# A local transformer's attention: squares of queries and keys in two operations, and the probabilities turned and emptied ahead of the values' projections

## The reference

```python
qkv = x @ Wqkv                              # shifted tokens
q = l2norm(q) * qs;  k = l2norm(k) * ksc    # t / max(norm(t), 1e-12), per head
q = q * cos * scale + rotate_half(q) * sin * scale
k = k * cos * inv   + rotate_half(k) * sin * inv
sim  = einsum('bhwie,bhwje->bhwij', q, look(k)) * 8.0   # this window and the one before
attn = softmax(where(mask, -max, sim), -1)
out  = einsum('bhwij,bhwje->bhwie', attn, look(v))
x = out @ Wo + x
# feed-forward, on shifted tokens again:
xn = (x - mu) / sqrt(var + 1e-05) * g + bln
a, gate = split(xn @ W1 + b1);  x = (a * gelu(gate)) @ W2 + b2 + x
```

## Time and profile before

| | |
|---|---|
| median of 3 runs | 2661.72 us (2658.05 to 2662.82) |
| the profiled execution | 2664.8 us |
| its span, first to last instruction | 2663.0 us |
| busy share of the span | PE 92%, PEld 73%, DVE 81%, ACT 74%, POOL 58% |
| mean granted clock of PE | 0.986 of full speed |

### The profile page before, as it was taken

How to read it: one execution, slowest core, us unless ns; L and a number is a source line. 1 busy time by engine, 2 the same in 40 slices (tenths; PEclk the granted TensorE clock), 3 DMA queues, 4 the chain that set the end, 5 groups by cost and what they waited for, 6 DMA issues and landing times. The chain is left out here.

```text
span 2663.0 us, 118331 instructions
## 1 busy us (share of the span) xinstructions
PE 2454.4 (92%) x52349; PEld 1956.3 (73%) x52349; DVE 2152.0 (81%) x2455; ACT 1983.5 (74%) x3935; POOL 1534.9 (58%) x1075
## 2 busy tenths in 40 slices
PE   6799999999999999999999999679999989997999
PEld 2478788888777788788887787557776767775787
DVE  5788888888788888888887787388888988885888
ACT  4678888888787888888887887566767666764776
POOL 3788887888778878887887777022223222322011
PEclk9899999999999999999999999899999999999999
DMA  3243433343334333434442333031322222221221
GB/s 95 55 93 90 104 76 91 90 105 79 88 89 104 76 91 92 106 78 95 93 107 62 83 83 80 25 72 36 74 52 66 46 64 53 62 49 37 81 71 42
DMA packets 275791, 201.99 MB, mean 76 GB/s; under 512 B 117568, under 2 KB 215880, under 8 KB 274248
## 3 DMA queue, kind: packets, MB, share of 16 engines
q1 hardware_dynamic: 275280, 194.42, 30.5%
HBM read 36.96 MB, written 1.11 MB: 14 GB/s over the span
## 5 line engine op out<-in xcount | busy, mean ns | idle before, releaser
L509 POOL TENSOR_TENSOR lt_t_sin<-lt_qk,lt_tab 128x512 f32<-128x512 f32 x384 | 685.0, 1804 | 261.2 <-DVE lt_qk L1274 258.7
L514 POOL TENSOR_TENSOR lt_qr<-lt_qr,lt_t_sin 128x1024 f32<-128x1024 f32 x192 | 455.7, 2373 | 28.7 <-PE bank L604 1.4
L2043 DVE TENSOR_REDUCE fa_neg_max<-bank 128x1 f32<-128x1024 f32 x256 | 301.5, 1219 | 94.1 <-PE bank L1851 93.4
L1267 DVE TENSOR_REDUCE lt_ssq<-lt_qr 128x32 f32<-128x2048 f32 x96 | 219.4, 2285 | 142.9 <-ACT lt_qr L976 142.9
L1875 PE MATMUL bank<-fa_prob_t,fa_v 32*64 32x128 f32 x16384 | 280.6, 275 | 31.0 <-issue 26.5
L2053 DVE STREAM_TRANSPOSE fa_prob_t<-fa_prob 128x1024 f32<-128x1024 f32 x256 | 302.0, 1218 | 0.0
L1875 PEld LDWEIGHTS bank<-fa_prob_t,fa_v 32*64 32x64 f32 x16384 | 242.5, 131 | 78.5 <-issue 57.2
L1965 ACT ACTIVATE fa_prob<-bank,fa_neg_max 128x1024 f32<-128x1024 f32 x128 | 142.5, 1114 | 207.8 <-DVE fa_neg_max L2043 161.6
L602 PE MATMUL bank<-lt_w_high,lt_x_high 128*128 128x512 f32 x576 | 280.4, 487 | 1.6 <-ACT lt_v_tok L995 1.3
L619 PE MATMUL bank<-ident,lt_qr 128*128 128x128 f32 x1536 | 234.6, 276 | 30.6 <-ACT lt_q_t L1010 18.9
L1274 DVE TENSOR_TENSOR lt_qk<-lt_qk,lt_rn 128x2048 f32<-128x2048 f32 x96 | 234.9, 2447 | 33.2 <-ACT lt_rn L989 32.3
(11 more groups left out here) (259 smaller groups left out, 5832.4 us busy)
## 6 DMA issues: line engine op xcount, KB each, us to landing
lt_v<-lt_v_tok SPq DMA_DIRECT2D x576, 128.0 KB, 2.4
fa_v<-fa_v_tok SPq DMA_DIRECT2D x256, 128.0 KB
lt_v<-lt_v_tok SPq DMA_DIRECT2D x192, 64.0 KB, 2.1
lt_k_t<-lt_k_t SPq DMA_DIRECT2D x84, 128.0 KB, 2.7
lt_v<-lt_v SPq DMA_DIRECT2D x168, 64.0 KB, 2.0
lt_w_raw<-in_lt_wqkv_dram SPq DMA_DIRECT2D x36, 256.0 KB, 3.6
ex_cw_all<-cw_kept SPq DMA_DIRECT2D x8, 1024.0 KB, 4.7
lt_x_s<-h_in SPq DMA_DIRECT2D x96, 64.0 KB, 2.8
```

Of the source, the lines that this page charges most:

```text
L509: pool.tensor_tensor(dst[:, :, i, :], src[:, :, 1 - i, :], tab[:, g // 2 % 2, 1, at:at + 32].unsqueeze(1).to_broadcast([P, HEADS, 32]), AL ...
L514: pool.tensor_tensor(qr[:, g % 2, half], qr[:, g % 2, half], t_sin[:, :], ALU.add).then_inc(S.rotated, 1)
L2043: dve.tensor_reduce(neg_max[:, u % 2, par:par + 1], bank[:, 2 * par:2 * par + 2, :].rearrange("p a n -> p (a n)"), AX.X, ALU.max, negate=T ...
```

## The change

On PE, both `turn_prob` of block i - 1 come right after `scores(i)`, ahead of both value projections, instead of between them. The table `uses` is reordered alike. On ACT, the square of the 2048 queries and keys of a block becomes two operations of 1024: the queries' half stands ahead of the emptying of the probabilities, the keys' half where the whole square was. The copy of the first values (`empty_v(i + 1, 0)`) moves behind the copies of the probabilities. The first half waits for the first two `qk` copies only and for the first two groups of turned `qr`; DVE's sum waits for both halves.

```diff
--- before.py
+++ after.py
@@ -275,13 +275,13 @@
                 uses["att", i - 2, 1] = len(uses)
             if i - 2 == ALL - 1:
                 uses["out", i - 2, 0] = len(uses)
+            if live(i - 1):
+                uses["prob", i - 1, 0] = len(uses)
+                uses["prob", i - 1, 1] = len(uses)
             if live(i + 1):
                 uses["v", i + 1, 0] = len(uses)
             if even(i, 6) is not None:
                 uses["down", even(i, 6), 0] = len(uses)
-            if live(i - 1):
-                uses["prob", i - 1, 0] = len(uses)
-                uses["prob", i - 1, 1] = len(uses)
             if live(i + 1):
                 uses["v", i + 1, 1] = len(uses)
             if even(i, 5) is not None:
@@ -919,6 +919,9 @@
                         last_mean(0)
                     if live(i):
                         scores(i)
+                    if live(i - 1):
+                        turn_prob(i - 1, 0)
+                        turn_prob(i - 1, 1)
                     if live(i + 1):
                         project_v(i + 1, 0)
                     if i == ALL + 2:
@@ -935,9 +938,6 @@
                     if i == ALL + 5:
                         last_mean(4)
                         last_var(4)
-                    if live(i - 1):
-                        turn_prob(i - 1, 0)
-                        turn_prob(i - 1, 1)
                     if live(i + 1):
                         project_v(i + 1, 1)
                     if live(i - 1):
@@ -969,11 +969,13 @@
                     act.wait_ge(S.proj, 4 * g + j + 1)
                     act.copy(qk[:, g % 2, j * CH:(j + 1) * CH], bank[:, turn_bank("qk", g, j), :]).then_inc(S.proj_out, 1)
 
-                def square_qk(g):
-                    act.wait_ge(S.proj_out, 4 * (g + 1))
+                def square_qk(g, a):
+
+                    half = slice(INNER * a, INNER * a + INNER)
+                    act.wait_ge(S.proj_out, 4 * g + 2 * a + 2)
                     if g >= 2:
-                        act.wait_ge(S.turned, 4 * (g - 1))
-                    act.activation(qr[:, g % 2, :], qk[:, g % 2, :], ACT.Square).then_inc(S.squared, 1)
+                        act.wait_ge(S.turned, 4 * (g - 2) + 2 * a + 2)
+                    act.activation(qr[:, g % 2, half], qk[:, g % 2, half], ACT.Square).then_inc(S.squared, 1)
 
                 def invert_norms(g):
 
@@ -1199,15 +1201,17 @@
                     for k in splits_at(i):
                         if k % WCH < 4:
                             split_high(k)
-                    if live(i + 1):
-                        empty_v(i + 1, 0)
+                    if live(i + 2):
+                        square_qk(i + 2, 0)
                     if live(i - 1):
                         empty_prob(i - 1, 0)
                         empty_prob(i - 1, 1)
+                    if live(i + 1):
+                        empty_v(i + 1, 0)
                     if even(i, 5) is not None:
                         shift_norm(even(i, 5))
                     if live(i + 2):
-                        square_qk(i + 2)
+                        square_qk(i + 2, 1)
                     if i == -1:
                         second_shift(2)
                     if i == 0:
@@ -1261,7 +1265,7 @@
             @blk.vector
             def _(dve):
                 def sum_squares(g):
-                    dve.wait_ge(S.squared, g + 1)
+                    dve.wait_ge(S.squared, 2 * (g + 1))
                     if g >= 2:
                         dve.wait_ge(S.clamped, g - 1)
                     dve.tensor_reduce(ssq[:, g % 2, :], qr[:, g % 2, :].rearrange("p (h d) -> p h d", d=HD), AX.X, ALU.add)\
```

## The result

The changed kernel takes 2626.61 us, median of 4 runs (2622.33 to 2628.85), beside 2662.27 for the kernel before on the same chip (4 runs, 2658.05 to 2664.34). The ratio is 0.9865, with a 95% interval of 0.9851 to 0.9879: 35.7 us less, where the prediction had summed 40. The profiled execution took 2627.98 us.

A forecast was written before the change was run, and what follows sets the result against it. The prediction took PE, 96% busy, as the bound, with waits before `weigh_v`, on ACT's loop and on POOL. Gains 25 + 22 - 7 = 40 us; 2664.8 - 40 - 3 (profiled run to median) = 2621.7 us, range 2606 to 2642.

The forecast's parts named there:

- The two waits named: PE's waits before `weigh_v` and, in even-i (D) steps, before the third transpose group, forecast to go: 25 and 22 us.
- The third: PE's wait for POOL's rotation before the third transpose group of odd-i (F) steps: 22 waits, 18.7 us, expected to remain.
- (b): On ACT, a half square of 1024 elements takes 0.92 us, bounds 0.90 and 1.03; the extra instruction costs 0.04.
- (c): Odd-i (F) step, S being the first value projection's start: second half square at S+2.76; ACT 1.04 us earlier afterwards.
- (d): PE's wait before `weigh_v` for the probabilities' copies goes: 0.29 us in F steps, 0.23 in D steps, 25 us altogether.
- (e): Even-i (D) step, third transpose group: PE's whole 0.62 us wait for ACT's `q_t` copy goes, 22 us over the run.
- (f): In 20 pairs with `split_low`, POOL, excluding DVE at a shared port, is late next: 0.33 us each, 7 us given back.
- (g): D step: `down` starts 0.78 us later, covered by DVE's 1.54 idle before the sum; uncovered, 38 us at worst.
- rival A: Only the wait before `weigh_v` pays and ACT's lead is lost: 2637 to 2644 us, say 2640; chance 0.17.
- Rival D: Slower: DVE's normalise starts before POOL's last rotation and blocks it, 30 us lost in 20 pairs, 2692 us; chance 0.06.
- B: More than summed: PE's waits for POOL go too, 9 us more, 56 in all, 2606 us; chance 0.08.
- C: No gain: the wait only moves, to the transposes behind the scores or the banks, 2662 us; chance 0.07.

The follow-up runs named there:

- order only: Kernel before with the new order of transposes and copies, but the square whole in its old place: 2654.73 us against 2668.93, ratio 0.9952.
- split only: Kernel before with the square in two halves, the first ahead of the first values' copy, all else in old order: 2638.39 us against 2668.93, ratio 0.9881.

## Why the prediction was right, and where its terms were off

- **The mechanism held.** The two waits named went, each with its own part of the change, as the waits of order only and split only show. The third stayed: PE's waits for POOL are 21 where 22 stood. DVE's idle before the sum is 0.52 each where about 0.6 was forecast, and in half of the steps it is gone.
- **(b)** took 0.92 for a half square and measured 0.95, inside its bounds.
- **(c)** was right to 0.05 us a step: S + 2.78, S + 3.73, S + 10.03 for 2.76, 3.68, 9.98.
- **(d) was mis-sized.** 0.52 us a pair were to go; 0.34 went (twice 0.09 over the usual spacing stays, though no engine is waited for), and 0.38 and 0.39 by order only. Its 25 us come to 14 (order only) or 16 (48 x 0.34).
- **(e) was mis-sized the other way**, as split only shows, 0.88 and 0.83 a pair for 0.62. A term was missing, and these rows suggest which: before, the weight load of the transposes that follow `project_out` stood some 0.2 us too, with no engine named, and after the change it doesn't. PE's weight loads there, before and after:

```profile
1049.18 0.42 PEld L619 LDWEIGHTS bank<-ident,lt_qr 128*128 128x128 f32 x4 [0.23 <-issue]
```
```profile
1027.94 0.47 PEld L619 LDWEIGHTS bank<-ident,lt_qr 128*128 128x128 f32 x4
```

   Such waits in front of L619 sum up to 16.9 us in 31 after and to 41.3 in 73 before; order only, without the split, has 40.1 in 61, and split only 14.6 in 33. So they go with the split. That they make up the missing 0.2 to 0.3 is argued from these rows; no experiment took it apart.
- **(f)** isn't settled in size. By the table split pairs gained as much as the others or a little less: 1.22 and 1.22 in the first profiles, 1.11 against 1.18 in the second. If only the 20 pairs that the prediction named count as split, it is 1.21 against 1.32 and 1.05 against 1.29. So 0 to 0.24 was given back a pair, not 0.33. In the pair shown, (f)'s own step didn't happen: the D step's normalise came at 1029.88, S + 10.15, 1.00 earlier than before and not 0.81, and took its usual 2.29. That the port costs more now is in DVE's rows all the same: in the steady part L1278 takes over 2.6 us 15 times before (14 in its second profile), 32 and 40 times after, most of it at the F step.
- **(g)** was right. DVE waits 66.6 us before `finish` instead of 26.1, and its wait for the square still shrank, so the D step's sum comes in time.
- **Where the rest went: rival A's mechanism, in part.** Clean pairs came out at 31.0 to 31.5 us, where 31.3 and 31.6 were forecast: 1.11 to 1.22 less than before. Over 48 pairs that would be over 50 us; 36 came. The pairs with a stall of PE that no engine causes, most of it inside `weigh_v`, gained less: 0.99 and 0.55 us in the first profiles, 0.36 and 0.19 in the second. The stalls themselves changed little: of the 38 in the profile before, 27 have one at the same place after, within two matmuls of it in the same step. Before and after:

```profile
1406.57 0.45 PE L677 MATMUL bank<-lt_v,lt_prob_t 64*32 64x64 f32 x28 [1.78 <-issue]
```
```profile
1381.77 0.45 PE L677 MATMUL bank<-lt_v,lt_prob_t 64*32 64x64 f32 x28 [1.85 <-issue]
...
1057.39 0.27 PE L677 MATMUL bank<-lt_v,lt_prob_t 64*32 64x64 f32 x2 [1.88 <-issue]
```

   Before, a pair with stalls took 0.2 to 0.8 us more than a clean one; after, 1.0 to 1.4. That fits PE's slack ahead of the third transpose group having absorbed part of a stall; no experiment tested it. This is A's mechanism, and it came beside the forecast's gains, not instead of them. The sum held part of it unawares, since it took (e) for 33 pairs and not for 48.
- **That 36 came out so near to 40 is in part luck.** (d) was too high by some 10 us. (e) was too low by some 20, if all pairs gained what the clean ones did (48 x 0.86 = 41 us for 22). What is over came off again in the pairs with stalls, which the sum left out.
- **One sign of being wrong came, and it was badly chosen.** A pair above 32 us anywhere in the steady part was to refute the prediction. After the change 24 of the 43 pairs are above 32 (22 in the second profile), where all 43 were before. In each profile all but two of those hold a stall. The sign took no account of the stalls that the earlier trace rows already showed. The other sign, the row of `weigh_v` almost empty, came, but most of its time only moved to the row "issue".
- **Rival D was put in the wrong place.** I looked at the D step's normalise and counted 3.8 us until it would start ahead of POOL's last rotation. It is the F step's that comes near, and there 1.57 us were left before and 0.72 after in the pairs shown. So the 0.06 for it rested on a margin that wasn't there, though the forecast held.
- **B** didn't come: POOL's waits stayed. **C** is out, as the time fell.

What stays open: why PE stalls at these matmuls (the DMA share is 0.00 in the window below in which it stands, and no engine is named), and what the 0.09 us before `weigh_v` is that remains.

## What to carry to other kernels

When a change takes time out of a loop between two engines, list for every other pair of engines which one comes first and by how much, and do it at each place in the step where both meet: a lead that shrinks is a price not yet paid, and doubling one small operation shows how far it is. Slack that nobody seems to need may be what absorbs stalls (here the pairs fit that, untested); count them into the new path before summing. And try the parts alone: here each removed just one wait, and yet was worth 0.7 and 1.4 times what the rows gave for it. And when a row of waits goes, look for its time under another name before you count it as won.

## What the runs showed of the hardware

PE's granted clock fell to half around some of its waits. In the changed kernel, around the stall at 1057.39 above (stretch, length, busy of PE, PEld, DVE, ACT, POOL, granted clock, DMA share and GB/s):

```profile
1056.00:1057.00 1.00, 0.00 (x0) 0.00 (x0) 1.00 (x1) 0.98 (x3) 1.00 (x2) 1.00 0.00 0
1057.00:1058.00 1.00, 0.61 (x4) 0.43 (x4) 0.58 (x2) 0.85 (x1) 1.00 (x2) 0.91 0.00 0
1058.00:1059.00 1.00, 1.00 (x4) 0.82 (x3) 0.46 (x1) 0.00 (x0) 0.86 (x2) 0.50 0.13 29
...
1061.00:1062.00 1.00, 1.00 (x6) 0.78 (x5) 0.27 (x1) 0.47 (x1) 0.78 (x2) 0.89 0.62 135
1062.00:1063.00 1.00, 1.00 (x11) 1.00 (x10) 0.54 (x2) 0.81 (x2) 0.00 (x0) 1.00 0.70 195
```

PE stands still for 1.88 us, works again, and its clock goes to 0.50, 1.2 GHz, until 1061, then back. The pairs that hold such a spell take 34.81 to 36.38 us in this profile. In the kernel before 28 of 43 pairs held stalls and the clock fell in one of them, in its second profile in none of 31; in the changed kernel in six of 27, in its second profile in one of 26. In the changed kernel with the doubled `split_low` it fell in 14 pairs. Around the wait of 3.67 us above:

```profile
548.00:549.00 1.00, 0.00 (x0) 0.00 (x0) 1.00 (x1) 0.00 (x0) 1.00 (x1) 0.76 0.72 199
549.00:550.00 1.00, 0.41 (x2) 0.41 (x3) 1.00 (x1) 0.00 (x0) 0.86 (x2) 0.50 0.95 170
...
554.00:555.00 1.00, 1.00 (x5) 0.71 (x4) 0.00 (x0) 0.58 (x1) 0.86 (x2) 0.50 0.00 0
```

Here the clock fell (0.76 from 548 to 549) while PE still stood. The pairs with a split and no stall took 34.40 and 34.73 us where the clock stayed (2 pairs) and 36.70 where it fell (median of 9). So of the 70 us that doubling cost there, some 15 x 3.2 = 48 are an estimate for the port's turned order (34.56 less 31.36 a pair), and the rest would be the clock's. The length of the wait alone doesn't decide it: waits of 3.11, 3.12 and 3.30 us on POOL (at 1130.73, 785.77 and 481.83) left the clock full, another of 3.12 us (at 821.74) did not, nor did stalls of 1.78 and 1.88 us.
